# First attention: the steps of a unit in which the next head is projected, and the maxima of steps 2 and 3

## The reference

```python
Q = (x @ Wq.T + bq).reshape(B, N, H, HD)          # H, HD = 16, 64; N = 2048
K = (x @ Wk.T + bk).reshape(B, N, H, HD)
V = (x @ Wv.T + bv).reshape(B, N, H, HD)
scores = jnp.einsum('bnhd,bmhd->bhnm', Q, K) * (SCALE * adaptive_scale)[None, :, None, None]
w = jax.nn.softmax(scores, axis=-1)
attn = jnp.einsum('bhnm,bmhd->bnhd', w, V).reshape(B, N, H * HD)
y = x + (attn @ Wo.T + bo)                         # then layer norm, gamma, beta
```

## Time and profile before

| | |
|---|---|
| median of 3 runs | 2480.86 us (2479.13 to 2484.33) |
| the profiled execution's own time | 2484.54 us |
| its span, first to last instruction | 2482.7 us |
| mean granted TensorE clock | 0.974 |
| busy: TensorE, VectorE, ScalarE, POOL | 89%, 70%, 69%, 58% |
| first attention, about | 60 to 1615 us of the span |

### The profile page before, as it was taken

How to read it: one execution, slowest core, us unless ns; L and a number is a source line. 1 busy time by engine, 2 the same in 40 slices (tenths; PEclk the granted TensorE clock), 3 DMA queues, 4 the chain that set the end, 5 groups by cost and what they waited for, 6 DMA issues and landing times.

```text
span 2482.7 us, 47718 instructions
## 1 busy us (share of the span) xinstructions
PE 2204.1 (89%) x17317; PEld 1696.9 (68%) x17317; DVE 1730.8 (70%) x3019; ACT 1714.3 (69%) x2160; POOL 1435.3 (58%) x794
## 2 busy tenths in 40 slices
PE   5889889898888988888889989867999999999998
PEld 3666666666666666666666666645788887788786
DVE  6777777777778677677687777676666665666652
ACT  3888888788788788788788888822545544545554
POOL 5787787787788778778778778812312311312300
PEclk7999999999999999999999999987999999999999
DMA  4000000000000000000000000010000000000000
GB/s 98 1 1 1 1 1 2 2 2 1 2 1 1 2 1 1 2 1 2 2 1 1 1 1 1 1 43 1 1 1 1 1 1 2 1 1 1 1 1 17
DMA packets 15276, 13.06 MB, mean 5 GB/s; under 512 B 3120, under 2 KB 14384, under 8 KB 14768
## 3 DMA queue, kind: packets, MB, share of 16 engines
q1 hardware_dynamic: 15024, 9.72, 1.4%
HBM read 8.67 MB, written 1.05 MB: 4 GB/s over the span
## 4 chain that ended last, share of the span: by engine, by line
issue 35%; PE 34%; POOL 16%; DVE 11%; ACT 3%; POOLq 0%; SPq 0%; DMA 0%; DVEq 0%; ACTq 0%
POOL PAB L450 11%; PE RING L1215 5%; PE ST L1319 4%; PE OO L1458 3%; PE ST L1320 3%; PE OO L1269 3%; DVE maxes L874 3%; POOL F L510 2%; POOL QL L434 2%; PE OO L1270 1%; PE RING L1411 1%; PE RING L1195 1%; PE RING L1236 1%; PE ST L1481 1%; PE RING L1391 1%
## 5 line engine op out<-in xcount | busy, mean ns | idle before, releaser
L450 POOL TENSOR_TENSOR PAB<-PR,PAB 128x1024 f16<-128x1024 f32 x512 | 1096.4, 2144 | 327.7 <-ACT PAB L636 309.8
L874 DVE TENSOR_REDUCE maxes<-RING 128x1 f32<-128x512 f32 (+1 forms) x1344 | 879.6, 670 | 349.1 <-PE RING L1215 228.1
L634 ACT ACTIVATE PR<-ST,lift 128x1024 f32<-128x1024 f32 x512 | 569.7, 1113 | 279.8 <-PE ST L1320 240.2
L636 ACT ACTIVATE PAB<-ST,lift 128x1024 f16<-128x1024 f32 x512 | 566.3, 1106 | 0.0
L1215 PE MATMUL RING<-KH,QL 128*128 128x512 f32 x1024 | 459.3, 455 | 103.9 <-DVE maxes L874 97.1
L1269 PE MATMUL OO<-VP,PAB 128*128 128x130 f16 x4096 | 497.4, 224 | 12.2 <-POOL PAB L450 11.0
L1319 PE MATMUL ST<-QL,KH 128*128 128x512 f32 x1024 | 452.8, 442 | 50.3 <-DVE QH L886 32.7
L1269 PEld LDWEIGHTS OO<-VP,PAB 128*128 128x128 f16 x4096 | 361.2, 98 | 196.0 <-issue 127.0
L1270 PE MATMUL OO<-VP,PAB 128*128 128x66 f16 x4096 | 463.3, 193 | 0.0
L1320 PE MATMUL ST<-QH,KL 128*128 128x512 f32 x1024 | 405.0, 396 | 0.0
L1270 PEld LDWEIGHTS OO<-VP,PAB 128*128 128x128 f16 x4096 | 370.5, 99 | 11.0 <-issue 10.0
(11 more groups left out here) (141 smaller groups left out, 2958.7 us busy)
## 6 DMA issues: line engine op xcount, KB each, us to landing
X<-in_L_attn_a_x SPq DMA_DIRECT2D x4, 256.0 KB, 3.5
SHARED<-in_rope_cos SPq DMA_DIRECT2D x1, 1024.0 KB, 4.8
SHARED<-in_rope_sin SPq DMA_DIRECT2D x1, 1024.0 KB, 7.0
out<-X SPq DMA_DIRECT2D x4, 256.0 KB, 2.3
RAW<-in_L_attn_a_Wq SPq DMA_DIRECT2D x1, 512.0 KB, 7.0
RAW<-in_L_attn_a_Wk SPq DMA_DIRECT2D x1, 512.0 KB, 8.2
RAW<-in_L_attn_a_Wv SPq DMA_DIRECT2D x1, 512.0 KB, 6.3
RAW<-in_L_attn_a_Wo SPq DMA_DIRECT2D x1, 512.0 KB, 7.2
```

The source lines that it names most:

```text
L450: pool.tensor_tensor(PB[:, s, :], PR[:, step % 2, :], PA[:, s, :], ALU.subtract).then_inc(p_low_pool, 1)
L634: act.activation(PR[:, step % 2, :], ST[step % 2][:, :], ACT.Exp, bias=lift[:, :])
L636: act.activation(PA[:, step % SLOTS_A, :], ST[step % 2][:, :], ACT.Exp, bias=lift[:, :]).then_inc(sa.exps, 1)
L874: dve.reduce_max(maxes[:, qt, c:c + 1], bank[:, 0:width], X_AXIS).then_inc(s.ring_taken, 1)
```

## The change

The blocks and the values of the next head are projected in steps 1 and 5 of a unit and no longer in 3 and 7, so that step 7 has the rows alone. All that follows a block or a half of the values moves along: ScalarE's pieces from the steps 4 to 7 and 0 to 3 to the steps 2 to 5, and 6, 7, 0, 1; the low parts on VectorE and POOL from the steps 5 and 1 to 3 and 7. Of the 16 maxima step 2 now has three and step 3 two; this holds for all units.

```diff
-HEAD_STEPS = (3, 7)
+HEAD_STEPS = (1, 5)
...
-        at = [0, 3, 5, 7, 10, 12, 14, 16, 16]
+        at = [0, 3, 5, 8, 10, 12, 14, 16, 16]
         items += [("max", i) for i in range(at[step], at[step + 1])]
```

## The result

The changed kernel takes 2617.19 us (median of 5 runs, 2612.14 to 2618.07) against 2481.43 us for the kernel before (5 runs). The ratio is 1.054, 95% interval 1.053 to 1.056: 136 us slower. The forecast was 2576 with a range of 2505 to 2625, so the side was right and the size, 95 us, was 41 us short.

The account below looks back on a forecast made before the run. No engine was full; ScalarE's pace or waits on other engines bound the steps. Chain +49 us and clock +46 us on the profiled 2484.5 us gave 2579.5, less 3.7 for the runs' median: 2576 us, range 2505 to 2625.

Parts of the forecast that it names:

- Part 1: Step 2 of every unit: the third maximum waits behind VectorE's normalisation; units 3 and 7 +2.3 us each.
- E2 to E3: ScalarE's first exponential of step 2 to that of step 3: forecast 4.4 to 5.5 us in every unit.
- Rival (b): Faster: in step 2 the third maximum costs nothing, as VectorE has normalised before TensorE asks; about 2420 us, chance 0.09.
- Part 2: Blocks in steps 1, 5: keys' low part hidden in step 3, delays rows in step 7, +1.1 us, four units.
- E0': ScalarE's first exponential of the next unit, forecast 6.9 us after step 6's in block units, 5.0 in values units.
- Part 3: Values in steps 1 and 5: POOL is free in step 6, unit's end falls from 7.62 to 5.0 us.
- The sum of the chain: All eight units' step distances added: +6.15 us a turn, +49 us in all.
- Part 4: TensorE's clock falls after longer pauses in steps 2 and 7: 40 more falls at 1.15 us, +46 us.
- (a): The chain of waits as forecast, with TensorE's clock nearly as before: 2530 us, chance 0.25.
- Rival (e): TensorE's clock falls after each of twelve pauses a turn, 83 more than now: 2625 us, chance 0.07.
- (c): Much slower: in step 6 of block units small operations miss the gap before POOL's subtraction; 2576 + 90 us, chance 0.08.
- (d): The stalls fall into unseen slack and nothing is left beyond 5 us: 2480 us, chance 0.04.

Follow-up runs that it names:

- e11: Kernel before with only the third maximum moved to step 2, plus five filling matmuls ahead of it in TensorE's pause: 2547.63 us, ratio 1.027.
- e1: Kernel before with only the maxima changed, three in step 2 and two in step 3; head work stays in steps 3 and 7: 2632.96 us, ratio 1.060.
- e2: Kernel before with only the head work moved, to steps 1 and 5; maxima stay two in step 2, three in step 3: 2538.12 us, ratio 1.022.
- e7: Kernel before with head work in steps 1 and 5 and the keys' low part behind the ring items in step 7 alone: 2481.79 us, ratio 0.999.
- e5: Changed kernel with unread matmuls filling TensorE's pauses, ahead of step 2's third maximum and at step 7's end in block units: 2523.76 us, ratio 1.017.
- e6: Kernel before with head work in steps 1 and 5 and the keys' low part behind the ring items in steps 3 and 7: 2454.81 us, ratio 0.988.
- e15: e6 with ten filling matmuls at the loop's end, step 3's low part ahead of unit 5's turned output, behind unit 0's step 4 items: 2426.49 us.
- e10: e6 with the keys' low part ahead of the turned output in units that turn an output in step 3: 2447.50 us, ratio 0.986.

## Why the prediction was right in its side and short in its size

**Part 1, the third maximum: right in kind.** E2 to E3 in unit 3 without the clock is 5.34 us. The forecast has 5.45, though its own terms, 2.35, 0.6 and 2.45, add up to 5.40. In unit 1 the changed kernel has 4.38 against 4.90 forecast, and in units 2 and 6 it has 3.98, below the 4.4 to 5.5 that the new profile should have shown everywhere. Rival (b) put the third maximum at 13.9 us a turn; with the head work where it was and the pauses filled (e11) it is 7.3, a middle turn of 204.2 against 196.9. As a whole it costs 65 us there, where the expectation of e1 had some 72.

**Part 2, the blocks: right at the end of a unit, right in step 3 only thanks to part 1.** E6 to E0' is 6.89 against 6.9. That step 3 hides the low part holds in the changed kernel, where two maxima stand behind it: E3 to E4 in unit 1 is 2.80 us. With three (e2, e7) it doesn't: in e2 it is 4.86.

**Part 3, the values: right.** E6 to E0' in unit 2 is 4.60 us against the 5.0 forecast.

**The sum of the chain,** +49, was measured as 38 to 42, by the run with the pauses filled. Its middle turn is 201.7 us, 4.8 more than the 196.9 before, where +6.15 was forecast; in both the clock is low for 4.0 us of a turn. The filling itself may cost a little of that, as in unit 1, where E2 to E3 is 4.69 us with it and 4.38 without.

**Part 4, the clock: the term was put at 46 us and measured 93.** What was mis-sized is the price of one fall, 1.15 us, and not the number of falls. Windows of the kernel after, before, and with the pauses filled:

```profile
200.00:1400.00 1200.00, 1032.75 (x8679) 769.09 (x8679) 783.52 (x1278) 910.77 (x968) 870.14 (x438) 0.93 0.01 2
...
200.00:1400.00 1200.00, 1064.87 (x9398) 783.11 (x9397) 894.60 (x1391) 984.92 (x1050) 944.24 (x476) 0.99 0.01 2
...
200.00:1400.00 1200.00, 1121.90 (x9614) 837.41 (x9613) 828.61 (x1354) 963.25 (x1023) 923.91 (x465) 0.99 0.01 2
```

The traces give every fall by itself. In the loop the kernel before has 8, the changed kernel 51, so 43 more where 40 were forecast, and e5 has 5. From the changed kernel to e5 that is 46 falls fewer for 93 us, 2.0 us for one. The forecast took each fall as 3.3 us long, but 20 of the 51, those in units 3, 5 and 7, last 6.8 us, as in the row 995.20:1001.90 above. And it counted on slack of 0.5 us a step, where a fall here meets the very scores that the wait has just released: from 242 to 24 us of low clock in the loop the time fell by 93 us, so 0.43 us for each of the 218 and not 1.15 / 3.3 = 0.35.

That the number of falls came out is luck. The rate of six in ten was taken over short and long pauses together. In the six middle turns the clock fell after each of the 36 pauses of 2.5 to 2.9 us (step 2 of units 3 and 7, step 7 of units 0, 1, 4 and 5) and after none of the 36 of 1.3 to 1.7 us (step 2 of the other units).

**The rivals.** (a), the chain alone with the clock nearly as before, at 2530, describes e5 (2524), not the change. Rival (e), a fall after each pause at 0.07, came nearest with 2625, but by two errors that cancel: it has 83 more falls at 1.15 us, and there are 43 more at 2.0. (c) is out: the small operation L879 takes 0.16 us in all units after the change. (d) is out by the waits themselves.

**The rival faster (b)** is out by e1 and e11: the third maximum isn't free. What it said of the change without it, 2420, isn't borne out as it stands: e2, the kernel without that maximum, has 2538. Only with the low part behind the items too do e6 and e15 lie below the kernel before.

## What to carry to other kernels

Look at what an in-order queue puts ahead of the item that releases the next stage: moving a cheap operation one place ahead of it costs its whole wait, and here (e1 and e11, 150 us of which 65 are the chain) more than twice that, since TensorE's clock was low for the matmuls that came right after the pause. When a change lengthens pauses of TensorE, cost each by the chain and again by a fall of the clock on the critical matmuls; a few matmuls that nobody reads, put ahead of the wait, tell the two apart in one run. A move that looks bad as a whole can hide a good one: the new steps for the head work were worth 31 us once the low part stood behind the items (e6, 2454.81 against 2485.96).

## What the runs showed of the hardware that was not expected

In the loop of the changed kernel the clock fell to 0.50, for 3.4 or 6.8 us, after 50 of the 53 pauses of TensorE that were longer than 2.2 us. The Trainium skill (TensorE: Matmul & The Clock Gate, "What's actually happening") says that the low clock is the default and that activity releases it. The trace agrees for these pauses, while the clock stayed at 1.00 after the 36 shorter ones above. The length of a pause doesn't settle it, though: in run e2 the same pause of 2.4 to 2.5 us was followed by a fall in 2 of 8 turns at the end of unit 0, and in all 8 at the end of unit 1 (2.4 to 2.7 us). What tells them apart wasn't shown. Filling the pauses kept the clock at 0.976 in the changed kernel.

VectorE's operation with two inputs in SBUF, the keys' low part (0.69 us at its fastest), waited for POOL's in every placement: its median is 1.5 to 2.1 us in all runs. In unit 0 of run e10 it waited for two of POOL's in a row, the second of which had started 0.77 us after it was issued: 3.45 us. In unit 5 of the same run POOL had a gap of 0.1 us and VectorE got in: 1.03 us. The Trainium skill (SBUF — State Buffer, "Who interferes with whom") says that a VectorE instruction with two SBUF inputs contends with a GpSimd instruction that reads SBUF, and that the order of issue decides who blocks. The runs agree that one waits for the whole of the other: the low part ends 0.55 us behind POOL's operation in both fences above. The order they don't bear out in unit 0 of e10, where POOL's second operation started later and yet went first. Why it did was not tried further.
